# Second group's sigmoids as 1/(1+exp(-x)), with its first attention one to two beats later and the exponential's table loaded ahead

## The chip, the core and the metric

The kernel runs on one core of a Trainium2 chip. The metric is the device time of one execution in microseconds. Five engines work side by side, each through its own instruction list in order, and meet at semaphores: TensorE (PE, its weight loads PEld), VectorE (DVE), ScalarE (ACT), GpSimd (POOL) and SyncE (SP, DMA issues).

## What is computed

One pre-norm decoder layer over x of 32 batches x 128 tokens x 128 features, with a context of 32 x 128 x 96:

```python
x = x + attn(layernorm(x))            # linear attention, 16 heads
x = x + xattn(layernorm(x), ctx)      # softmax cross attention, 16 heads of 64
x = x + ffn(layernorm(x))             # shared SwiGLU + top-1 of 8 experts
# attn:
h = x @ Wh + bh;  v = x @ Wv + bv
q = sigmoid(x @ Wq + bq);  k = sigmoid(x @ Wk + bk)
kv = einsum('bndh,bnmh->bdmh', k, v)
num = einsum('bndh,bdmh->bnmh', q, kv)
den = einsum('bndh,bdh->bnh', q, k.sum(tokens))
out = relu((layernorm(num / den) * ln_w + ln_b) * (h + beta) @ Wo + bo)
```

## The kernel before

The 32 batches are eight **groups** of four. The first attention ("s1") is done for a whole group at once, in named steps; the cross attention is done batch by batch. The program's time is a list of **beats** (n, b), n from -7 to 31 and b from 0 to 3. In the four beats of n, batch n's probabilities are turned (the transposes, L1386) and batch n+1's scores and exponentials are made. Every engine's list is written out by the same loop over (n, b); what it issues in a beat, and in which order, is fixed there.

In a beat TensorE issues: the turn of a quarter of batch n's probabilities (`turn_probs`), products for v, q and k of coming batches, at b = 0 the scores of batch n+1 and the product of batch n-1's probabilities with V, at b = 2 the output product of batch n-1, and last the s1 steps of the beat. VectorE issues: the reciprocals of the softmax sums, the emptying of v and of half of the q and k banks, the row maxima (`row_max`, L860), and last its s1 steps. ScalarE issues the emptying of turned probabilities (L1117), four exponentials with sums for each quarter (`exp_chunk`, L1111), the other half of q and k, and last its s1 steps. GpSimd normalises probabilities (`norm_probs`, L599) and does s1's rsqrt by power, the normalisations, and the "gate terms".

The s1 steps of a group g run, in order of need: stats of x; rstd of x; normalise x; turn x; copy x^T and x^T low (a number is held as a high and a low part for the products); project first pair and second pair (h, k and v of two batches each into `hkv`); project q; sigmoids (ScalarE, on the k part of `hkv`, L1082, and from the bank of q into `qsT`, L1086); k^T v; mask; q k^T v; attention (VectorE: a reciprocal of the denominators L743, two products L745, and the statistics); rstd of attention; gating, first half (L756) and second half (L763); turn gated; copy gated^T; output; x1 (L775, L778 and statistics); rstd of x1; normalise x1; turn x1; x1^T high (ScalarE, L1092) and x1^T low (VectorE, L794). The last two feed the q products of the next pair of batches of the cross attention: for group 1 those of batches 4 and 5, first at beat (2, 0).

Tables `PE_S1`, `ACT_S1`, `DVE_S1` and `POOL_S1` give each step a place relative to the group's start; the dictionary `MOVED` overrides it. Group 0 runs before the cross attention starts. Group 1's s1 lies where the cross attention begins, at beats (-2, 3) to (1, 2). Groups 2 to 7 have theirs inside the steady cross attention.

Matmul results go to eight PSUM banks: four for the scores, four in a ring (`Ring`) that everything else takes in program order. A result can start only when the tenant four places before has been emptied, by VectorE or ScalarE.

`sigmoid` and `exp` are in different activation tables, so that ScalarE's list has an ACT_TABLE_LOAD at each change. `sh_gu_hi` (ScalarE, L1150) and `sh_gu_lo` (VectorE, L1011) are the parts of the feed-forward weights, first used at beat (6, 0). `stay_awake` (L1451) issues matmuls with no use for their result in the stretches before the cross attention.

Of the kernel before, what the change touches and what calls it, by code (L numbers as in the profile page):

```python
# [10 lines left out]
ALU = mybir.AluOpType  # L11
ACT = mybir.ActivationFunctionType
AX = mybir.AxisListType

P = 128


class Ring:
# [17 lines left out]
    def made(self, name):  # L36
        return self.ready, self.index[name] + 1
# [18 lines left out]
def decoder_layer(nc, x, ctx_in, Wh, bh, Wq, bq, Wk, bk, Wv, bv, beta, ln_w, ln_b, Wo, bo,  # L56
# [30 lines left out]
    with ctx:  # L87
        def sb(name, shape, dt=F32):
            return ctx.enter_context(nc.sbuf_tensor(name, shape, dt))

        def sem(name):
            return ctx.enter_context(nc.semaphore(name))
# [9 lines left out]
        wkvh_lo = sb("wkvh_lo", [P, 3 * D], F32R)  # L102
        wo = sb("wo", [P, D])
        bq_col = sb("bq_col", [P, 1])
        b_hkv = sb("b_hkv", [P, 3 * D])
        beta_bc = sb("beta_bc", [P, D])
        lnw_bc = sb("lnw_bc", [P, D])
# [153 lines left out]
        centred = [sem("x_centred"), sem("x1_centred")]  # L261
        normed = [sem("x_normalised"), sem("attention_gated"), sem("x1_normalised")]
        k_sig = sem("k_sigmoid")
        hi_in = [sem("ctxT_high_part"), sem("x1T_high_part")]
        gate_in = sem("gate_terms")
        x1_in = sem("x1_ready")
# [74 lines left out]
                 (0, "turn context"): (-6, 2), (0, "context high"): (-6, 2), (0, "context low"): (-6, 2),  # L341
                 (0, "residual"): (-3, 0),
                 (1, "stats of x"): None, (1, "rstd of x"): (-4, 2), (1, "normalise x"): (-4, 3),
                 (1, "turn x"): (-2, 3), (1, "copy x^T"): (-2, 3), (1, "x^T low"): (-2, 3),
                 (1, "project first pair"): (-1, 0), (1, "first pair"): (-1, 0),
                 (1, "project second pair"): (-1, 1), (1, "second pair"): (-1, 1)})

        def steps_at(table_, starts, n, b):

            return [(g, step) for g, a in enumerate(starts) for (slot, beat), step in table_.items()  # L350
                    if MOVED.get((g, step), (a + slot, int(beat))) == (n, b)]
# [326 lines left out]
        def _(dve):  # L678
# [28 lines left out]
            def s1(g, step):  # L707
# [15 lines left out]
                if step in ("first pair", "second pair"):  # L723
                    for u in ((1, 2) if step == "first pair" else (3, 4)):
                        ps = made(r1, (g, u))
                        if u == 1 and g > 0:

                            dve.wait_ge(gate_in, g)
                        nc.vector.tensor_tensor(hkv[:, u - 1, 0:3 * D], ps[:, 0:3 * D], b_hkv[:], ALU.add)\
                            .then_inc(r1.emptied["s1_dve"], 1)  # L730
                if step == "mask":
                    for u in (6, 7):
                        ps = made(r1, (g, u))
                        for j in range(2):
                            last = nc.vector.tensor_tensor(kvm[:, 2 * (u - 6) + j, :],
                                                           ps[:, j * KVW:(j + 1) * KVW], head_mask[:], ALU.mult)
                        last.then_inc(r1.emptied["s1_dve"], 1)
# [236 lines left out]
            for n in range(FIRST, B):  # L974
                for b in range(NC):
# [28 lines left out]
                    if (n, b) == (FIRST + 2, 2):  # L1004
# [1 line left out]
                        nc.vector.scalar_tensor_tensor(out=xwq_lo[:], in0=rawq, scalar=DH ** -0.5,  # L1006
                                                       in1=xwq_hi[:].bitcast(F32), op0=ALU.mult,
                                                       op1=ALU.subtract).then_inc(w_lo, 1)
                    if (n, b) == (-1, 3):
                        dve.wait_ge(wm_hi, 1)  # L1010
                        nc.vector.tensor_tensor(sh_gu_lo[:], rawgu, sh_gu_hi[:].bitcast(F32), ALU.subtract)\  # L1011
                            .then_inc(wm_lo, 1)
                    if (n, b) == (FIRST + 2, 2):
                        dve.wait_ge(w_hi, 3)
                        nc.vector.tensor_tensor(xwv_lo[:], rawv, xwv_hi[:].bitcast(F32), ALU.subtract)\
                            .then_inc(w_lo, 1)
                    for g, step in steps_at(DVE_S1, S1_AT, n, b):
                        if g == 0 and step == "first pair":
                            dve.wait_ge(consts, CONSTS_BIAS)
                        if g == 0 and step == "mask":  # L1020
                            dve.wait_ge(consts, CONSTS_S1)
                        s1(g, step)
# [48 lines left out]
        def _(act):  # L1071
            def made(ring, name):
                act.wait_ge(*ring.made(name))
                return ring.bank(name)

            def s1(g, step):
                if step == "copy x^T":
                    nc.scalar.copy(xnT_hi[:], made(r1, (g, 0))[:]).then_inc(xT_hi, 1)
                if step == "sigmoids":

                    act.wait_ge(*r1.freed((g, 4)))
                    nc.scalar.activation(hkv[:, :, D:2 * D], hkv[:, :, D:2 * D], ACT.Sigmoid).then_inc(k_sig, 1)  # L1082
                    ps = made(r1, (g, 5))
                    if g == 0:
                        act.wait_ge(bq_in, 16)
                    nc.scalar.activation(qsT[:], ps[:], ACT.Sigmoid, bias=bq_col[:]).then_inc(r1.emptied["s1_act"], 1)  # L1086
                if step == "copy gated^T":
                    nc.scalar.copy(gT[:], made(r1, (g, 10))[:]).then_inc(r1.emptied["s1_act"], 1)
                if step == "context high":
                    nc.scalar.copy(ctxT_hi[:, g % 2], made(r1, (g, 13))[0:DE, :]).then_inc(hi_in[0], 1)  # L1090
                if step == "x1^T high":
                    nc.scalar.copy(xn2T_hi[:, g % 2], made(r1, (g, 12))[:]).then_inc(hi_in[1], 1)  # L1092

            def ffn(g, step):
                ring = ffn_ring(g)
# [49 lines left out]
            nc.scalar.copy(wq_hi[:], rawq1).then_inc(w1_hi, 1)  # L1145
            for n in range(FIRST, B):
                for b in range(NC):
                    if (n, b) == (-1, 2):
                        act.wait_ge(wm_in, 16 * 4)
                        nc.scalar.copy(sh_gu_hi[:], rawgu).then_inc(wm_hi, 1)  # L1150
                    if live(n):
# [77 lines left out]
        def _(pe):  # L1229
# [28 lines left out]
            def s1(g, step):  # L1258
# [17 lines left out]
                if step == "project q":  # L1276
                    product3(claim(r1, (g, 5))[:], wq_hi[:], wq_lo[:], xnT_hi[:], xnT_lo[:]).then_inc(r1.ready, 1)
                if step == "k^T v":
                    pe.wait_ge(k_sig, g + 1)
                    for u in (6, 7):  # L1280
                        ps = claim(r1, (g, u))
                        for j in range(2):
                            b = 2 * (u - 6) + j
                            last = pe.matmul(ps[:, j * KVW:(j + 1) * KVW], hkv[:, b, D:2 * D], hkv[:, b, 2 * D:],
                                             start=True, stop=True)
                        last.then_inc(r1.ready, 1)
                if step == "q k^T v":

                    pe.wait_ge(*r1.freed((g, 5)))
                    for u in (8, 9):  # L1290
                        ps = claim(r1, (g, u))
                        pe.wait_ge(*r1.freed((g, u - 2)))
                        for j in range(2):
                            b = 2 * (u - 8) + j
                            last = pe.matmul(ps[:, j * KVW:(j + 1) * KVW], qsT[:, b * S:(b + 1) * S], kvm[:, b, :],
                                             start=True, stop=True)
                        last.then_inc(r1.ready, 1)
# [280 lines left out]
```

## Time and profile before

| | |
|---|---|
| median of 3 runs | 607.21 us (606.89 to 608.82) |
| the profiled execution's own time | 606.39 us |
| its span in the trace | 604.7 us |
| PE busy | 576.7 us (95%), 5479 matmuls |
| PEld busy | 528.7 us (87%) |
| DVE busy | 432.2 us (71%), 1210 instructions |
| ACT busy | 432.0 us (71%), 1514 instructions |
| POOL busy | 311.9 us (52%) |
| chain that ended last, by engine | PE 66%, ACT 16%, DVE 10% |
| ACT_TABLE_LOAD | L1111 x8 and L1082 x7 and L1142 x1, mean 1283 ns |

The busy shares are means over the whole span; matmuls overlap, and their ends are modelled. Start times are microseconds from the span's start. Where an engine runs back to back, the step from one start to the next is a little shorter than the busy length of an instruction. A row "x4" stands for four instructions in a row, with the time from the first start to the last end. The profiled execution is 1.7 us longer than its span.

### The profile page before, as it was taken

The page shows a single profiled execution, that of the slowest core. Times are in us where ns is not written, and L with a number is a line of the kernel's source. Part 1 is how long each engine was busy: PE and PEld are TensorE (multiplying, and loading weights), DVE is VectorE, ACT ScalarE, POOL GpSimd, SP SyncE. Part 2 cuts the span into 40 slices and gives each one's busy share as a digit, 9 for nine tenths or more (in the row PEclk, how much of TensorE's full clock was granted, in tenths as well). Part 3 has the DMA queues.
Part 4 walks back from the last instruction along what each step waited for, and adds up shares of the span by engine and source line. Part 5 has one row for each costly group of instructions (what it writes and reads, how often), then busy time and mean ns, then how long its engine had stood idle before and what let it go on. Part 6 is the DMA issues. An engine that isn't in the chain of part 4 may idle for free.

```text
span 604.7 us, 15181 instructions
## 1 busy us (share of the span) xinstructions
PE 576.7 (95%) x5479; PEld 528.7 (87%) x5479; DVE 432.2 (71%) x1210; ACT 432.0 (71%) x1514; POOL 311.9 (52%) x332
## 2 busy tenths in 40 slices
PE   8978999999999999999999999999999999899993
PEld 8867998988999899989998889989998988788993
DVE  4869666877685858776876787767856558589773
ACT  2668778786877777677867687768777876665881
POOL 3545553365336643675347525655464326445774
PEclk9999999999999999999999999999999999999997
DMA  6530000100010000010000000000220201242530
GB/s 158 141 65 14 18 3 1 31 2 2 1 33 17 21 2 14 19 38 1 14 20 27 11 5 11 19 19 3 89 70 20 66 8 36 82 129 76 150 103 19
DMA packets 24955, 23.52 MB, mean 39 GB/s; under 512 B 7007, under 2 KB 22497, under 8 KB 24880
## 3 DMA queue, kind: packets, MB, share of 16 engines
q1 hardware_dynamic: 21520, 15.96, 10.2%
q0 software_dynamic: 2784, 6.32, 3.0%
q8 instruction: 45, 0.74, 0.5%
q10 hardware_dynamic: 576, 0.26, 0.2%
q14 instruction: 30, 0.25, 0.1%
HBM read 15.03 MB, written 7.95 MB: 38 GB/s over the span
## 4 chain that ended last, share of the span: by engine, by line
PE 66%; ACT 16%; DVE 10%; issue 2%; POOL 2%; DMA 2%; SPq 1%; POOLq 0%; DVEq 0%; ACTq 0%
PE bank L1408 8%; PE bank L1376 8%; PE bank L1397 8%; PE bank L1386 7%; PE bank L1237 7%; ACT prob L1111 7%; PE bank L1239 6%; PE bank L1238 6%; PE bank L1522 4%; PE bank L1539 2%; PE bank L1255 2%; PE bank L1357 2%; ACT probT L1117 2%; DMA prob<-in_L_xattn_Wk_dram 2%; PE bank L1243 1%
## 5 line engine op out<-in xcount | busy, mean ns | idle before, releaser
L1111 ACT ACTIVATE prob<-bank,mneg 128x128 f32<-128x128 f32 x512 | 183.4, 388 | 63.3 <-DVE mneg L860 63.1
L599 POOL TENSOR_TENSOR prob<-prob,rden 128x512 f32<-128x512 f32 x128 | 131.1, 1045 | 104.2 <-DVE rden L867 104.0
L1111 ACT ACTIVATION_READ_ACCUMULATOR prob<-bank,mneg 128x1 f32 x512 | 115.8, 226 | 0.0
L1117 ACT COPY probT<-bank 128x512 f32<-128x512 f32 x128 | 77.9, 609 | 19.3 <-PE bank L1386 18.7
L860 DVE TENSOR_REDUCE mneg<-bank 128x4 f32<-128x512 f32 x128 | 83.1, 670 | 2.5 <-PE bank L1376 2.5
L1386 PE MATMUL bank<-ident,prob 128*128 128x128 f32 x512 | 78.6, 276 | 3.4 <-POOL prob L599 2.0
L538 POOL TENSOR_TENSOR rstd<-var_eps,neg_half 128x4 f32<-128x4 f32 x24 | 24.7, 1030 | 97.5 <-DVE var_eps L694 97.5
L1386 PEld LDWEIGHTS bank<-ident,prob 128*128 128x128 f32 x512 | 59.6, 142 | 10.5 <-ACT probT L1117 3.1
L1376 PE MATMUL bank<-kT,qT 64*128 64x128 f32 x1024 | 66.2, 279 | 0.4 <-ACT prob L1111 0.4
L1376 PEld LDWEIGHTS bank<-kT,qT 64*128 64x128 f32 x1024 | 59.8, 188 | 6.3 <-issue 2.5
L1408 PE MATMUL bank<-xwo,oT 128*128 128x128 f32 x512 | 63.7, 277 | 0.5 <-ACT oT L1121 0.5
L877 DVE COPY V<-bank 128x512 f32<-128x512 f32 x62 | 42.8, 690 | 29.6 <-PE bank L1239 28.4
L1397 PE MATMUL bank<-probT,V 128*64 128x128 f32 x1024 | 63.0, 276 | 0.0
L1408 PEld LDWEIGHTS bank<-xwo,oT 128*128 128x128 f32 x512 | 59.8, 192 | 2.9 <-ACT qT L1131 1.2
L1397 PEld LDWEIGHTS bank<-probT,V 128*64 128x64 f32 x1024 | 55.2, 137 | 4.0 <-issue 0.3
L1522 PE MATMUL bank<-oT,qT 128*128 128x128 f32 x312 | 41.1, 275 | 0.0
L1522 PEld LDWEIGHTS bank<-oT,qT 128*128 128x128 f32 x312 | 38.0, 192 | 0.2
L591 POOL DMA_INDIRECT routed<-record,row_i x32 | 32.7, 1022 | 7.9 <-issue 4.8
L1121 ACT COPY oT<-bank 128x512 f32<-128x512 f32 x64 | 35.6, 601 | 1.2 <-PE bank L1397 0.3
L1237 PE MATMUL bank<-xwv_hi,ctxT_hi 96*128 96x512 f32 x64 | 30.7, 480 | 1.4 <-ACT oT L1121 1.3
L1131 ACT COPY qT<-bank 128x512 f32<-128x512 f32 x32 | 19.7, 616 | 16.5 <-PE bank L1239 16.5
L1237 PE MATMUL bank<-xn2T_hi,xwq_hi 128*128 128x256 f32 x96 | 28.9, 301 | 0.9 <-DVE V L877 0.6
(224 smaller groups left out, 1389.7 us busy)
## 6 DMA issues: line engine op xcount, KB each, us to landing
prob<-routed SPq DMA_DIRECT2D x39, 128.5 KB, 2.2
s_work<-in_x_dram SPq DMA_DIRECT2D x8, 256.0 KB, 2.9
ctx_nat<-in_ctx_dram SPq DMA_DIRECT2D x8, 192.0 KB, 2.7
routed<-blank SPq DMA_DIRECT2D x9, 128.5 KB, 4.1
s_work<-in_L_ffn_rt_gate_dram SPq DMA_DIRECT2D x1, 1024.0 KB, 5.5
s_work<-in_L_ffn_rt_up_dram SPq DMA_DIRECT2D x1, 1024.0 KB, 9.5
prob<-in_L_xattn_Wq_dram SPq DMA_DIRECT2D x1, 512.0 KB, 6.9
xwo<-in_L_xattn_Wo_dram SPq DMA_DIRECT2D x1, 512.0 KB, 9.2
```

Source lines behind the costliest of these rows:

```text
L599: nc.gpsimd.tensor_tensor(view, view, spread(rden[:, m % 2, c * NC:(c + 1) * NC], 2, S), ALU.mult)\
L860: nc.vector.tensor_reduce(mneg[:, m % 2, c * NC:(c + 1) * NC], score_bank[c][:].rearrange("p (h k) -> p h k", k=S), AX.X, ALU.max, negate= ...
L877: nc.vector.tensor_copy(V[:, m % 2, half * 512:(half + 1) * 512], ps[:])\
L1111: last = nc.scalar.activation(prob[:, m % 2, p * S:(p + 1) * S], score_bank[c][:, i * S:(i + 1) * S], ACT.Exp, bias=mneg[:, m % 2, p:p + 1 ...
L1117: nc.scalar.copy(probT[:, m % 2, c * 512:(c + 1) * 512], made(r1, ("T", m, c))[:])\
L1237: pe.matmul(ps, w_hi_, t_hi, start=True, stop=False)
L1238: pe.matmul(ps, w_hi_, t_lo, start=False, stop=False)
L1376: last = pe.matmul(score_bank[2 * j + half][:, i * S:(i + 1) * S], qT[rows, pair % 2, 4 * j + i, cols], kT[rows, pair % 2, 4 * j + i, cols ...
L1386: last = pe.transpose(ps[:, i * S:(i + 1) * S], prob[:, m % 2, p * S:(p + 1) * S], ident[:])
L1397: last = pe.matmul(ps[DH * half:DH * half + DH, i * S:(i + 1) * S], V[:, m % 2, h * DH:(h + 1) * DH], probT[:, m % 2, p * S:(p + 1) * S], ...
L1408: last = pe.matmul(ps[:, 0:D], oT[:, m % 2, k * S:(k + 1) * S], xwo[:, k, :], start=(k == 0), stop=(k == NK - 1))
L1522: last = pe.matmul(gu_bank[(j - 1) % 3][:, c * P:(c + 1) * P], w4[(j - 1) % 3][:, c * P:(c + 1) * P], recT[:, (j - 1) % 2], start=True, st ...
```

## The change

For group 1 alone the sigmoids become exponentials on ScalarE (of -x, the q bias negated in advance into `bq_neg`), and VectorE adds 1 and takes the reciprocal: two passes over 128x512 for k, two for q, in a step of its own, "second sigmoids", at beat (-1, 3). TensorE's k^T v and q k^T v of group 1 wait for the semaphore of that step. An exponential of 128x4 with no use for its result stands behind group 0's "x1^T high". Steps of group 1 are moved later (before, where they had no entry of their own, the tables gave the places in the second column):

| step of group 1 | before | after |
|---|---|---|
| x^T low | (-2, 3) | (-1, 0), behind two row maxima |
| sigmoids (ACT) | (-1, 1) | (-1, 2) |
| second sigmoids (DVE) | none | (-1, 3) |
| k^T v; mask | (-1, 2) | (0, 0) |
| gate terms (POOL) | (-1, 1) | (0, 0) |
| q k^T v; attention; rstd of attention | (-1, 3) | (0, 1) |
| gating, first and second half | (0, 0), (0, 1) | (0, 2) |
| turn gated; copy gated^T | (0, 2) | (0, 3) |
| output; x1; rstd of x1 | (0, 3) | (1, 0) |
| normalise x1 | (1, 0) | (1, 1) |
| turn x1; x1^T high; x1^T low | (1, 2) | (1, 3) |

`sh_gu_hi` goes from beat (-1, 2) to (-2, 2), `sh_gu_lo` from (-1, 3) to (1, 2). Groups 0 and 2 to 7 keep the sigmoid.

```diff
@@ MOVED
-                 (1, "turn x"): (-2, 3), (1, "copy x^T"): (-2, 3), (1, "x^T low"): (-2, 3),
+                 (1, "turn x"): (-2, 3), (1, "copy x^T"): (-2, 3), (1, "x^T low"): (-1, 0),
...
+                 (1, "sigmoids"): (-1, 2), (1, "k^T v"): (0, 0), (1, "mask"): (0, 0), (1, "q k^T v"): (0, 1),
+                 (1, "attention"): (0, 1), (1, "gate terms"): (0, 0), (1, "rstd of attention"): (0, 1),
+                 (1, "gating, first half"): (0, 2), (1, "gating, second half"): (0, 2),
+                 (1, "turn gated"): (0, 3), (1, "copy gated^T"): (0, 3), (1, "output"): (1, 0), (1, "x1"): (1, 0),
+                 (1, "rstd of x1"): (1, 0), (1, "normalise x1"): (1, 1), (1, "turn x1"): (1, 3),
+                 (1, "x1^T high"): (1, 3), (1, "x1^T low"): (1, 3)})
@@ VectorE
+                if step == "second sigmoids":
+                    dve.wait_ge(exp_1, 1)
+                    v = hkv[:, :, D:2 * D]
+                    link(nc.vector.tensor_scalar(v, v, 1.0, None, ALU.add))
+                    nc.vector.reciprocal(v, v).then_inc(sig_1, 1)
+                    dve.wait_ge(*r1.freed((g, 5)))
+                    link(nc.vector.tensor_scalar(qsT[:], qsT[:], 1.0, None, ALU.add))
+                    nc.vector.reciprocal(qsT[:], qsT[:]).then_inc(sig_1, 1)
...
-                    if (n, b) == (-1, 3):
+                    if (n, b) == (1, 2):
                         dve.wait_ge(wm_hi, 1)
...
+                    if (n, b) == (-1, 3):
+                        s1(1, "second sigmoids")
@@ ScalarE
+                if step == "sigmoids" and g == 1:
+                    act.wait_ge(*r1.freed((g, 4)))
+                    nc.scalar.activation(hkv[:, :, D:2 * D], hkv[:, :, D:2 * D], ACT.Exp, scale=-1.0).then_inc(exp_1, 1)
+                    ps = made(r1, (g, 5))
+                    act.wait_ge(bq_turned, 1)
+                    nc.scalar.activation(qsT[:], ps[:], ACT.Exp, scale=-1.0, bias=bq_neg[:])\
+                        .then_inc(r1.emptied["s1_act"], 1)
...
+                    if g == 0:
+                        nc.scalar.mul(bq_neg[:], bq_col[:], -1.0).then_inc(bq_turned, 1)
...
                     nc.scalar.copy(xn2T_hi[:, g % 2], made(r1, (g, 12))[:]).then_inc(hi_in[1], 1)
+                    if g == 0:
+
+                        nc.scalar.activation(table_first[:], neg_half[:], ACT.Exp)
...
-                    if (n, b) == (-1, 2):
+                    if (n, b) == (-2, 2):
                         act.wait_ge(wm_in, 16 * 4)
@@ TensorE
-                    pe.wait_ge(k_sig, g + 1)
+                    if g == 1:
+                        pe.wait_ge(sig_1, 1)
+                    else:
+                        pe.wait_ge(k_sig, max(g, 1))
...
-                    pe.wait_ge(*r1.freed((g, 5)))
+                    pe.wait_ge(*((sig_1, 2) if g == 1 else r1.freed((g, 5))))
```

## Rows read from the trace of the kernel before

**Rows 1.** Busy time by engine from 57.3 us to the last matmul. Columns: start and end, length, engines, TensorE clock
```profile
57.30:595.00 537.70, 527.53 (x5110) 484.22 (x5110) 390.94 (x1084) 398.46 (x1425) 281.72 (x280) 1.00 0.11 33
```

**Rows 2.** Chain that ended last, 38 to 46 us. Columns: start, length (us), engine, output, line
```profile
38.91 0.69 DVE mneg L860
...
39.62 2.90 ACT prob L1111 x16
...
42.53 1.28 ACT L1082
...
43.83 0.64 ACT s_work L1082
```

**Rows 3.** ScalarE in order of time, 35 to 46 us. Start, length, instruction, idle before
```profile
35.68 0.59 ACT L1131 COPY qT<-bank 128x512 f32<-128x512 f32 x1 [2.10 <-PE bank L1239]
37.12 0.58 ACT L1131 COPY qT<-bank 128x512 f32<-128x512 f32 x1 [0.85 <-PE bank L1239]
...
44.94 0.61 ACT L1150 CAST sh_gu_hi<-x 128x512 fp32r<-128x512 f32 x1
```

**Rows 4.** TensorE in order of time, 44 to 66 us
```profile
44.51 1.25 PE L1284 MATMUL bank<-s_work 128*128 128x144 f32 x8 [2.03 <-ACT s_work L1082]
...
47.03 0.60 PE L1386 MATMUL bank<-ident,prob 128*128 128x128 f32 x4
...
56.64 0.66 PE L1255 MATMUL bank<-ident,s_work 128*128 128x128 f32 x4 [0.67 <-DVE s_work L763]
57.24 0.66 PE L1386 MATMUL bank<-ident,prob 128*128 128x128 f32 x4
...
59.31 1.06 PE L1307 MATMUL bank<-wo,qsT 128*128 128x128 f32 x8
...
65.33 0.66 PE L1386 MATMUL bank<-ident,prob 128*128 128x128 f32 x4
```

**Rows 5.** VectorE in order of time, 45 to 57 us
```profile
45.31 1.01 DVE L735 TENSOR_TENSOR kvm<-bank,head_mask 128x144 f32<-128x144 f32 x4 [1.48 <-PE bank L1284]
46.24 1.05 DVE L1011 TENSOR_TENSOR sh_gu_lo<-x,sh_gu_hi 128x512 fp32r<-128x512 f32 x1
47.21 0.34 DVE L743 RECIPROCAL rden<-bank 128x32 f32<-128x32 f32 x1
...
50.29 0.20 DVE L867 RECIPROCAL rden<-den 128x8 f32<-128x8 f32 x1
50.41 0.64 DVE L872 COPY qT<-bank 128x512 f32<-128x512 f32 x1
50.96 1.28 DVE L860 TENSOR_REDUCE mneg<-bank 128x4 f32<-128x512 f32 x2
52.16 2.06 DVE L756 SCALAR_TENSOR_TENSOR s_work<-s_work,mv 128x128 f32<-128x128 f32 x4
...
55.45 1.13 DVE L763 SCALAR_TENSOR_TENSOR s_work<-s_work,rstd 128x128 f32<-128x128 f32 x4
56.50 0.68 DVE L789 TENSOR_TENSOR ctxT_lo<-bank,ctxT_hi 96x512 fp32r<-96x512 f32 x1
```

**Rows 6.** VectorE groups by line and shape. Columns: operation, count, busy us, mean ns, idle
```profile
L867 DVE RECIPROCAL rden<-den 128x8 f32<-128x8 f32 x64 | 12.5, 196 | 7.0 <-ACT prob L1111 6.4
...
L743 DVE RECIPROCAL rden<-bank 128x32 f32<-128x32 f32 x16 | 5.7, 354 | 3.0 <-PE bank L1295 3.0
...
L839 DVE TENSOR_TENSOR rank<-bank,next_row 128x32 f32<-128x32 f32 x8 | 1.5, 183 | 0.0
```

**Rows 7.** TensorE in order of time, 70 to 71.3 us
```profile
70.42 0.60 PE L1255 MATMUL bank<-ident,xn 128*128 128x128 f32 x4
```

**Rows 8.** ScalarE in order of time, 72.5 to 73.3 us
```profile
72.90 0.58 ACT L1131 COPY kT<-bank 128x512 f32<-128x512 f32 x1 [0.57 <-PE bank L1239]
```

**Rows 9.** TensorE in order of time, 590 to 605 us: its last matmuls
```profile
595.14 0.71 PE L1539 MATMUL bank<-kT,V 128*128 x4 [0.64 <-DVE V L1039]
```

**Rows 10.** Granted clock after the last matmul of the program
```profile
597.00:598.00 1.00, 0.00 (x0) 0.00 (x0) 0.00 (x0) 0.00 (x0) 0.69 (x2) 0.59 0.02 0
```

More of the change, by code:

```diff
@@ L104, in decoder_layer @@
         bq_col = sb("bq_col", [P, 1])
+        bq_neg = sb("bq_neg", [P, 1])
         b_hkv = sb("b_hkv", [P, 3 * D])
@@ L263, in decoder_layer @@
         k_sig = sem("k_sigmoid")
+        bq_turned = sem("q_bias_negated")
+        exp_1 = sem("second_group_exponentials")
+        sig_1 = sem("second_group_sigmoids")
         hi_in = [sem("ctxT_high_part"), sem("x1T_high_part")]
@@ L343, in decoder_layer @@
                  (1, "stats of x"): None, (1, "rstd of x"): (-4, 2), (1, "normalise x"): (-4, 3),
-                 (1, "turn x"): (-2, 3), (1, "copy x^T"): (-2, 3), (1, "x^T low"): (-2, 3),
+                 (1, "turn x"): (-2, 3), (1, "copy x^T"): (-2, 3), (1, "x^T low"): (-1, 0),
                  (1, "project first pair"): (-1, 0), (1, "first pair"): (-1, 0),
-                 (1, "project second pair"): (-1, 1), (1, "second pair"): (-1, 1)})
+                 (1, "project second pair"): (-1, 1), (1, "second pair"): (-1, 1),
+                 (1, "sigmoids"): (-1, 2), (1, "k^T v"): (0, 0), (1, "mask"): (0, 0), (1, "q k^T v"): (0, 1),
[4 more added lines that the diff above has]
+                 (1, "x1^T high"): (1, 3), (1, "x1^T low"): (1, 3)})
         def steps_at(table_, starts, n, b):
@@ L1078, in s1 @@
                     nc.scalar.copy(xnT_hi[:], made(r1, (g, 0))[:]).then_inc(xT_hi, 1)
-                if step == "sigmoids":
+                if step == "sigmoids" and g == 1:
[5 more added lines that the diff above has]
+                        .then_inc(r1.emptied["s1_act"], 1)
+                if step == "sigmoids" and g != 1:
                     act.wait_ge(*r1.freed((g, 4)))
```

## The prediction

> **What bounds the kernel now.** I read the busy time by stretch first. From 57.3 us to the last matmul TensorE is busy 527.5 of 537.7 us at full clock [rows 1]: what delays its list there by a microsecond delays the end by one, for nothing idle follows that could take it up. So the change is worth what it does to TensorE's position by the time the steady stretch starts. Ahead of that the bound changes. In the chain, ScalarE's first eight exponentials are followed by a table load, then by k's sigmoid, which TensorE's k^T v awaits [rows 2]; TensorE's own list shows the 2.03 us pause ahead of k^T v [rows 4]. VectorE's list from 45.3 us on is then without a gap, and TensorE waits for it again, 0.67 us, at turn gated [rows 4, 5]. VectorE is thus the next to be late, and the change gives it more work there.
>
> My marker is the start of the turn of batch 1's second quarter, at 65.33 us before [rows 4]. The same work must be done ahead of it in both kernels.
>
> **ScalarE's edits.** The exponential's early load (1.28 us) falls into an idle time of 2.10 us, `sh_gu_hi` at its new place (0.61 us) into one of 0.85 us [rows 3]; both are hidden, and without that cover would hold back the q copies behind them by their length. The negated bias is one tiny copy in group 0's idle start: nothing. x^T low goes behind two row maxima: the maxima come some 0.3 us earlier, the first pair 0.3 us later. The third exponential chunk waits for its row maximum, which is behind the first pair, until about 42.5; so the earlier start is not kept. Two of the chunks took 2.90 us [rows 2]. k's exponential is behind the third chunk: 42.5 + 1.45 + 0.65 = **44.6 us**, and it is only the input of the new VectorE step. k's sigmoid was done at 44.47 before [rows 2], so the removed load (1.28) has been spent on the chunk put ahead.
>
> Here row and page differ. The row has the load at 42.53 and the sigmoid at 43.83, so a switch costs 1.28 us and nothing after it [rows 2]. The Trainium skill, "ScalarE: Activation LUTs", What ACT_TABLE_LOAD costs, adds a drain of about 1.38 us to each; with it the two removed switches would free ScalarE for 5.3 instead of 2.6 us. The trace speaks against it, and ScalarE isn't the bound in what follows.
>
> **The new VectorE step.** Two additions and two reciprocals over 128x512. An addition is like any pass of that size, 0.65 (0.6 to the 1.05 of `sh_gu_lo`, both operands of which are in SBUF) [rows 5]. No reciprocal of that size is in the trace. It has one of 8 elements at 196 ns and one of 32 at 354 ns, while a product of 32 elements takes 183 ns [rows 6]. So the reciprocal costs by the element: (354 - 196)/24 = 6.6 ns, 196 + 504 x 6.6 = 3.5 us; or the excess over the product, 171/32 = 5.3 ns, x 512 + 0.65 = 3.4 us. The lower bound is a plain pass, 0.65; the upper takes the whole of the longer row as cost by the element, 354/32 = 11 ns, which gives 5.7 us. I take **3.4 us**, since both rows point there. The step is 2 x (0.65 + 3.4) = 8.1 us, and ends at 44.6 + 8.1 = **52.7 us**.
>
> The rule on this is in the Trainium skill, "VectorE: DVE Perf Modes", the 8-slice pipeline: reciprocal iterates with a repeat count of 8. Eight times the 1.05 ns an element of a plain pass would be 4.3 us, and the sum 1.8 us longer.
>
> **What is queued behind it.** In VectorE's order, with the start-to-start steps of [rows 5]: reciprocal of the sums 0.1, q copy 0.55, two row maxima 1.2, mask 0.95, V copy 0.6, row maximum 0.6, attention with its statistics 3.1 (47.21 to 50.29), context low 0.6, reciprocal, row maximum and q copy 1.3, gating 2.1 and 1.1. Together 12.2 us; gated values at **64.9 us**. TensorE keeps ahead of each: it waits for the q copy at 53.4 before the v product (the copy frees a bank), for the mask and the ring at q k^T v, for context low at the next v product. ScalarE's exponentials of batch 1 begin at 54, after the maximum.
>
> Turn gated was at 56.64, and from there TensorE ran back to back to the marker, 8.7 us. The turn, v and q products of beat (0, 3) (57.24 to 59.31, 2.1 us) are now ahead of turn gated, the output behind the scores and the product with V. What remains is 6.6 us [rows 4]: marker at 64.9 + 6.6 = 71.5, which is **6.2 us late**. That `sh_gu_lo` and the mask leave their old place is in this walk and counts no second time.
>
> **Behind the marker.** (a) x1 (two passes of 0.7 and statistics like those of attention, some 2.85 us) now begins at 71.5 and the V copy is behind it, so the output product of batch 0 waits for its bank: 71.5 + 2.85 + 0.6 = 74.95, while TensorE arrives at 74.4: 0.5 us. (b) Turn x1 was at 70.42, more than two microseconds before the k copy of 72.90 [rows 7, 8]. Now it is behind that k product, and x1^T high is on ScalarE behind k copy and an exponential chunk: 0.5 + 1.4 + 0.5 = 2.4 us, beside TensorE's two turns of 0.85. With x1^T low (0.7, against the 0.5 of products that need only the high part) the q product of beat (2, 0) waits **1.9 us**. This does not depend on the reciprocals.
>
> Moved otherwise: GpSimd's gate terms leave the way of the first normalisation, so the first turn comes before its 47.03 [rows 4]; that is lost again at the q copy's bank. SyncE's load of the third group's x waits for x1_in, so is issued some 11 us later, for use much further on: nothing.
>
> **Sum:** 6.2 + 0.5 + 1.9 = 8.6 us. 606.39 + 8.6 = 615.0; the median of the runs shown is 0.8 above the profiled execution, so **615.8 us**.
>
> **Rivals.** (1) Reciprocals are plain passes. Step 2.6 us, end at 47.3; VectorE's 12.2 then has some 0.6 of waits for TensorE: gated at 60.0, marker 66.6, 1.3 late, with (a) and (b) 3.7: 610.9. For it: nothing but the missing row; against it the 354 to 183 ns. Chance 0.10.
>
> (2) TensorE's clock falls. After k^T v (to 49.9) and one turn it idles from 50.3 to 53.4. After the last matmul of the program, which ended at 595.85, the granted clock was at full until the second from 597.0 to 598.0, whose mean is 0.59, between 2.4 and 1.2 GHz [rows 9, 10]: a pause of some 2 us was enough there. The v, q and q k^T v products that VectorE awaits (2.1 us) would take twice as long: 617.9 at most. Against: VectorE is behind on its own work, so much of that is hidden. Chance 0.13.
>
> (3) It is faster: the pause of 2.03 us goes, and nothing takes its place: 604.4, with the 0.8 605.2. Place: the marker, which must come before 65.3. It decides at turn gated, which must be ready by 65.3 - 6.6 = 58.7, so that VectorE's step ends by 46.5: 1.9 us for four passes. Even then (b) costs 1.9. It needs passes at under 0.5 us and the k copy, exponentials and x1^T high hidden. Chance 0.04.
>
> (4) The exponential's table stays loaded where it was, as the early activation doesn't bring it ahead. The load was hidden behind the row maximum (ready at 39.60, exponential at 39.62) [rows 2], so this changes nothing: 615.8, in the forecast's chance.
>
> **The numbers.** Forecast 0.70, 613 to 618 by itself (reciprocals at 2.9 to 4.3 us give -1.0 to +1.8). Passes partly hidden so that the time stays within 0.3% (1.8 us, about what a measurement of this kernel can tell from no change) 0.03. Range: down to rival 1 less a little, up to rival 2 with the longer reciprocals: 609.8 to 619.0. Slower takes forecast, rivals 1 and 2: 0.93.
>
> **What would show it.** Two reciprocals of 128x512 near 3.4 us on VectorE, ending near 52.7; TensorE's k^T v at about 48.8 and then pauses; turn gated at 64.9; marker at 71.5; a wait of almost 2 us for x1^T high near 80; then the old list 8 to 9 us late to the end, with TensorE's sum of work unchanged. Wrong would be: reciprocals under 1 us, a marker before 66, or no wait for x1^T high.

## The result and the profile after

The changed kernel takes 617.16 us (median of 4 executions, 616.99 to 619.04), the kernel before 607.47 in the same runs. The ratio is 1.0167, 95% interval [1.0143, 1.0190]: slower by 9.7 us. The forecast was 615.8, the range 609.8 to 619.0. The spans of the two profiled executions are 615.3 and 604.7 us, 10.6 us apart.

VectorE in order of time, changed kernel. Columns: start, busy length, engine, line, operation, idle before:

```profile
45.04 0.43 DVE L746 TENSOR_SCALAR s_work<-s_work 128x512 f32<-128x512 f32 x1 [0.50 <-ACT s_work L1103]
45.50 3.35 DVE L747 RECIPROCAL s_work<-s_work 128x512 f32<-128x512 f32 x1
48.77 0.36 DVE L749 TENSOR_SCALAR qsT<-qsT 128x512 f32<-128x512 f32 x1
49.17 3.35 DVE L750 RECIPROCAL qsT<-qsT 128x512 f32<-128x512 f32 x1
52.44 0.14 DVE L887 RECIPROCAL rden<-den 128x8 f32<-128x8 f32 x1
52.50 0.63 DVE L892 COPY qT<-bank 128x512 f32<-128x512 f32 x1
...
61.30 2.04 DVE L776 SCALAR_TENSOR_TENSOR s_work<-s_work,mv 128x128 f32<-128x128 f32 x4
63.38 1.14 DVE L783 SCALAR_TENSOR_TENSOR s_work<-s_work,rstd 128x128 f32<-128x128 f32 x4
```

The new step takes 7.5 us, from 45.0 to 52.5. Its first row waits 0.50 us for ScalarE's exponential; behind it no row in the list down to the gated values at 64.5 has any idle time ahead of it. The gating passes that answer to [rows 5] were at 52.16 and 55.45.

TensorE, who waited for whom, 40 to 90 us of the changed kernel. Columns: waiting instruction, releaser, us in total, times, longest:

```profile
PE bank L1289 <- DVE s_work L783: 2.7, 1, 2.7
PE bank L1423 <- POOL prob L611: 2.0, 1, 2.0
PE bank L1277 <- ACT xn2T_hi L1123: 1.8, 1, 1.8
PE bank L1271 <- DVE qT L892: 1.4, 1, 1.4
...
PE bank L1445 <- DVE V L897: 0.6, 1, 0.6
```

TensorE in order of time, changed kernel:

```profile
64.57 1.12 PE L1289 MATMUL bank<-ident,s_work 128*128 128x128 f32 x4 [2.72 <-DVE s_work L783]
...
73.66 0.60 PE L1423 MATMUL bank<-ident,prob 128*128 128x128 f32 x4
...
77.44 2.05 PE L1445 MATMUL bank<-xwo,oT 128*128 128x128 f32 x16 [0.63 <-DVE V L897]
...
83.99 0.36 PE L1277 MATMUL bank<-xn2T_hi,xwq_hi 128*128 128x256 f32 x1 [1.77 <-ACT xn2T_hi L1123]
```

The marker of the prediction, the turn of batch 1's second quarter, is at 73.66, against 65.33 in [rows 4]: 8.33 us late. Behind it stand the two new waits, 0.63 us for the output product's bank and 1.77 us for x1^T high. 8.33 + 0.63 + 1.77 = 10.7 us, which is the difference of the spans (10.6) but for 0.1.

The profiled executions don't all reach this part of the program at the same time. The first q copy on ScalarE, which no edit delays, starts at 35.68 us in the kernel before [rows 3] and at 35.95 in the changed kernel, so 0.27 of the 8.33 us are a later start. In other runs it starts up to 1.5 us later; where it bears on a comparison below, it is given.

TensorE needs 9.1 us from turn gated to the marker, where the same instructions took 6.6 before (65.33 - 56.64, less the 2.07 us of products that now stand ahead of turn gated [rows 4]). The changed kernel's busy time by stretch says why (columns as in [rows 1]; the third from the end is the granted clock):

```profile
46.00:48.00 2.00, 2.00 (x15) 1.78 (x16) 2.00 (x1) 1.45 (x7) 0.37 (x1) 0.51 0.00 0
...
62.00:64.00 2.00, 0.00 (x0) 0.00 (x0) 1.96 (x6) 1.88 (x9) 0.67 (x1) 0.78 0.00 0
64.00:66.00 2.00, 1.43 (x7) 1.43 (x8) 1.23 (x4) 0.27 (x1) 0.69 (x1) 0.50 0.00 0
66.00:68.00 2.00, 2.00 (x11) 1.78 (x11) 0.14 (x1) 0.90 (x2) 1.34 (x2) 0.50 0.00 0
68.00:70.00 2.00, 2.00 (x20) 2.00 (x22) 0.69 (x2) 0.00 (x0) 0.00 (x0) 0.52 0.00 0
```

TensorE is idle from 61.9 to 64.6, its clock falls to 1.2 GHz in that pause, and it runs at half until about 70: 2.5 us of the lateness. It is at half from 46 to 49.5 us too, behind the 2.0 us pause of the first turn; there TensorE waits for VectorE afterwards in any case, 1.4 us for the q copy.

So the loss of the profiled execution is the start's 0.3 us and four terms of the change: turn gated 5.6 us late by VectorE's list, 2.5 us half clock, 0.6 us a bank, 1.8 us x1^T high.

### The profile page after: what moved, and what is told of

Read it like the earlier page. It is cut to its first block, busy times and chain, and to the rows that moved or that the text cites. A ratio compares the mean times of both kernels' runs of the same rounds, so it can differ in the third digit from the quotient of the medians.

```text
span 615.3 us, 15187 instructions
## 1 busy us (share of the span) xinstructions
PE 580.3 (94%) x5479; PEld 532.0 (86%) x5479; DVE 439.5 (71%) x1214; ACT 430.5 (70%) x1514; POOL 312.4 (51%) x332
## 4 chain that ended last, share of the span: by engine, by line
PE 66%; ACT 15%; DVE 12%; issue 2%; DMA 2%; POOL 2%; SPq 1%; POOLq 0%; DVEq 0%; ACTq 0%
PE bank L1413 8%; PE bank L1445 8%; PE bank L1434 7%; PE bank L1423 7%; ACT prob L1145 7%; PE bank L1271 7%; PE bank L1273 6%; PE bank L1272 5%; PE bank L1559 4%; PE bank L1289 2%; PE bank L1576 2%; PE bank L1394 2%; DMA prob<-in_L_xattn_Wk_dram 2%; ACT probT L1151 2%; PE bank L1277 2%
## 5 line engine op out<-in xcount | busy, mean ns | idle before, releaser
L1413 PE MATMUL bank<-kT,qT 64*128 64x128 f32 x1024 | 68.1, 285 | 0.0
L1413 PEld LDWEIGHTS bank<-kT,qT 64*128 64x128 f32 x1024 | 62.0, 194 | 6.0 <-issue 3.0
```

The costliest lines, as they stand in the source:

```text
L1413: last = pe.matmul(score_bank[2 * j + half][:, i * S:(i + 1) * S], qT[rows, pair % 2, 4 * j + i, cols], kT[rows, pair % 2, 4 * j + i, cols ...
```

## The experiments

Times of the first four stand against 607.33 us of the kernel before, of the next four against 607.30, of the last four against 607.09.

### Eighteen wake matmuls in the pause ahead of turn gated

```diff
+                    if (n, b) == (0, 3):
+                        pe.wait_ge(exp_done, NC + 1)
+                        stay_awake(18)
```

> The changed kernel with 18 matmuls of no use (120 ns each, 2.2 us) in TensorE's pause of 2.7 us ahead of turn gated. Theory (the half clock from 64 to 69.5 us is a cost of its own): the clock stays at 2.4 GHz, the marker (turn of batch 1's second quarter, 73.66) comes near 71.4, the time is about 2.3 us under the changed kernel's 617.2, at 614.9. Rival (VectorE and the chain of waits set the pace there, the half clock is covered): within 0.3 us of 617.2.

619.28 us, 1.0186 [1.0165, 1.0207]. A miss. The 18 matmuls show as 36 instructions in the trace:

```profile
63.74 4.18 PE L1488 MATMUL bank<-ident 128*128 128x128 f32 x36
67.76 0.60 PE L1289 MATMUL bank<-ident,s_work 128*128 128x128 f32 x4
```

The clock stays full there, and turn gated to marker takes 74.32 - 67.76 = 6.6 us. But turn gated is 3.2 us later than in the changed kernel. 0.8 us of it is a later start. 1.2 us is the wake matmuls, which end after the gated values are ready (66.6). The remaining 1.2 us has a cause ahead of the edit, where the instructions are those of the changed kernel: here the clock stays full at the first turn and falls at the next pause.

```profile
53.98 0.50 PE L1271 MATMUL bank<-xwv_hi,ctxT_hi 96*128 96x512 f32 x1 [2.60 <-DVE qT L892]
...
57.05 2.09 PE L1332 MATMUL bank<-kvm,qsT 128*128 128x144 f32 x8
```

```profile
56.00:58.00 2.00, 2.00 (x11) 2.00 (x10) 1.17 (x2) 2.00 (x11) 1.97 (x2) 0.50 0.04 8
```

Q k^T v takes 2.09 us instead of 1.15, and VectorE's attention (58.24) waits 1.07 us for it. This is what rival 2 of the prediction described. At the marker these two terms of 1.2 us use up the 2.5 us that the full clock gives. The clock falls once more from 86.25 to 89.75 us, behind the wait for x1^T high; the start and this fall are the 2.3 us by which this span exceeds the changed kernel's. The run says nothing on the net worth; it was repeated with ten, below.

### Without q's reciprocal

```diff
-                    link(nc.vector.tensor_scalar(qsT[:], qsT[:], 1.0, None, ALU.add))
-                    nc.vector.reciprocal(qsT[:], qsT[:]).then_inc(sig_1, 1)
+                    nc.vector.tensor_scalar(qsT[:], qsT[:], 1.0, None, ALU.add).then_inc(sig_1, 1)
```

> The changed kernel without q's reciprocal (q is left as 1+exp(-x), so this part of the computation is changed). Theory (VectorE's list is in series from the new step to turn gated): the step ends 3.35 us earlier, near 49.2, turn gated near 61.2, the time 3.3 us under 617.2, at 613.9 with the clock still falling in the pause, near 611.7 if the pause ahead of turn gated gets short enough. Rival (ScalarE's exponentials or the PSUM ring hold TensorE, and VectorE is late beside them): under 1 us gained, over 616.2.

613.68 us, 1.0104 [1.0089, 1.0118]: 3.5 us under the changed kernel, for a reciprocal of 3.35 us. The profiled execution is the slowest of the four (616.07; the others 613.30 to 614.00). TensorE in it:

```profile
61.25 1.11 PE L1288 MATMUL bank<-ident,s_work 128*128 128x128 f32 x4 [2.73 <-DVE s_work L782]
...
70.78 0.60 PE L1422 MATMUL bank<-ident,prob 128*128 128x128 f32 x4
```

Turn gated moves from 64.57 to 61.25, by 3.32 us, and the pause ahead of it stays 2.7 us, so the half clock comes again (9.5 us to the marker). Up to turn gated the series on VectorE holds one for one. At the end only 1.0 us of it is left in this execution, as the clock falls again at the wait for x1^T high and is at half until 84.75:

```profile
82.00:84.00 2.00, 2.00 (x16) 1.78 (x16) 0.69 (x1) 0.00 (x0) 1.99 (x2) 0.50 0.02 4
```

The mean granted clock of the other three is 0.989 to 0.992, of this one 0.986; they spent less time at half, and no trace shows where. That the medians differ by the length of the reciprocal is thus partly luck.

### Turn x1 back by one beat

```diff
-                 (1, "rstd of x1"): (1, 0), (1, "normalise x1"): (1, 1), (1, "turn x1"): (1, 3),
-                 (1, "x1^T high"): (1, 3), (1, "x1^T low"): (1, 3)})
+                 (1, "rstd of x1"): (1, 0), (1, "normalise x1"): (1, 1), (1, "turn x1"): (1, 2),
+                 (1, "x1^T high"): (1, 2), (1, "x1^T low"): (1, 2)})
```

> The changed kernel with turn x1, x1^T high and x1^T low of group 1 back at beat (1, 2). Theory (the 1.77 us wait for x1^T high comes from its place behind the exponentials): that wait goes, but turn x1 now waits for GpSimd's normalisation, which ended at 80.1 where TensorE arrives near 79.3: net 0.8 to 1.2 us under 617.2, at 616.2. Rival (the x1 chain is late as such, and the wait only changes its name): within 0.3 us of 617.2.

615.89 us, 1.0142 [1.0123, 1.0161]: 1.3 us under the changed kernel. TensorE's waits in this run have no x1^T high, and instead:

```profile
PE bank L1289 <- POOL xn L557: 0.7, 1, 0.7
```

1.77 - 0.68 = 1.1 us, as expected: most of that wait came from the place of the step and not from a late x1.

### All moves, with ScalarE's sigmoid

```diff
-                    nc.scalar.activation(hkv[:, :, D:2 * D], hkv[:, :, D:2 * D], ACT.Exp, scale=-1.0).then_inc(exp_1, 1)
+                    nc.scalar.activation(hkv[:, :, D:2 * D], hkv[:, :, D:2 * D], ACT.Sigmoid).then_inc(sig_1, 1)
...
-                    nc.scalar.activation(qsT[:], ps[:], ACT.Exp, scale=-1.0, bias=bq_neg[:])\
+                    nc.scalar.activation(qsT[:], ps[:], ACT.Sigmoid, bias=bq_col[:])\
...
-                    if (n, b) == (-1, 3):
-                        s1(1, "second sigmoids")
```

> All of the moves kept, but group 1's sigmoids done by ScalarE as before, so no additions and reciprocals on VectorE and two table loads back. Theory (the moved places cost by themselves, the reciprocals come on top): ScalarE's last chunk of batch 0 ends near 49.5 instead of 46.5, VectorE goes on from there instead of 52.4, everything some 3 us earlier; with the clock not falling late 5 us: 612 to 614.3, still clearly over the kernel before at 607.4. Rival (the reciprocals are the whole loss): within 1 us of 607.4.

617.65 us, 1.0161 [1.0145, 1.0178] (one execution of the six took 1972 us and is left out of the ratio; without it the median is 617.51). Both the theory's 612 to 614.3 and the rival's 607.4 are missed: without any reciprocal it is as slow as the changed kernel. ScalarE and TensorE of this run, in order of time, and the stretch between them:

```profile
44.65 1.28 ACT L1101 ACT_TABLE_LOAD   x1
...
47.17 1.28 ACT L1143 ACT_TABLE_LOAD   x1
```

```profile
50.02 2.08 PE L1411 MATMUL bank<-kT,qT 64*128 64x128 f32 x16 [1.17 <-ACT prob L1143]
52.03 1.85 PE L1319 MATMUL bank<-s_work 128*128 128x144 f32 x8
```

```profile
48.00:50.00 2.00, 0.85 (x8) 0.56 (x6) 0.00 (x0) 1.99 (x10) 0.00 (x0) 0.50 0.00 0
50.00:52.00 2.00, 1.98 (x16) 1.79 (x16) 1.95 (x4) 1.05 (x4) 1.71 (x2) 0.50 0.00 0
```

The loads hold the last exponentials of batch 0 back to 49.9, the second half of batch 1's scores waits for them, and all of it runs at half clock, so that k^T v is at 52.03 (50.06 in the changed kernel) and gating ends at 64.5 again. VectorE idles 5.3 us here instead of doing reciprocals. What had been left out of the expectation is the half clock and the scores' wait for the last exponentials. The half clock holds from 46.25 to 53.5 us, longer than in the changed kernel. In these places the table loads and the half clock together thus cost as much as the reciprocals; how it divides between the two was not separated. What the moves cost without either is shown further down.

### Ten wake matmuls

```diff
-                        stay_awake(18)
+                        stay_awake(10)
```

> The changed kernel with 10 wake matmuls ahead of turn gated. In the first try 18 of them showed as 36 instructions and took 4.2 us, longer than the pause; 10 take 2.3 us of the 2.7. Theory (the half clock after the pause costs by itself): the clock stays full from 62 us on, turn gated to the marker takes 6.6 us instead of 9.1, the time is 2 to 2.5 us under 617.2. Rival (the lost half clock is paid elsewhere, as the clock falls at another pause): within 1 us of 617.2.

615.79 us, 1.0136 [1.0119, 1.0152]: 1.4 us under the changed kernel, between theory and rival. TensorE of this run:

```profile
61.03 2.39 PE L1488 MATMUL bank<-ident 128*128 128x128 f32 x20
63.92 0.66 PE L1289 MATMUL bank<-ident,s_work 128*128 128x128 f32 x4 [0.49 <-DVE s_work L783]
...
70.53 0.60 PE L1423 MATMUL bank<-ident,prob 128*128 128x128 f32 x4
```

Turn gated to marker takes 6.6 us. The marker is 3.1 us earlier than in the changed kernel, 0.7 us of it by an earlier start and 2.5 us by the clock. But now the clock falls behind the wait for x1^T high:

```profile
82.00:84.00 2.00, 2.00 (x25) 1.98 (x26) 1.25 (x2) 0.00 (x0) 1.76 (x2) 0.70 0.01 4
84.00:86.00 2.00, 2.00 (x22) 1.78 (x20) 1.93 (x11) 1.51 (x8) 0.00 (x0) 0.50 0.03 8
```

In the changed kernel's own trace the same wait of 1.77 us brought no fall. So both hold: the half clock at turn gated is a cost of its own, 2.5 us at the marker, and in this execution a part of it is paid at another pause, as the rival said.

### Tanh in the moved places

`v` and `qsT` become tanh(x/2) + 1, twice the sigmoid; the factor cancels between numerator and denominator. `bq_neg` holds half the bias.

```diff
-                    nc.scalar.activation(hkv[:, :, D:2 * D], hkv[:, :, D:2 * D], ACT.Exp, scale=-1.0).then_inc(exp_1, 1)
+                    nc.scalar.activation(hkv[:, :, D:2 * D], hkv[:, :, D:2 * D], ACT.Tanh, scale=0.5).then_inc(exp_1, 1)
...
-                    link(nc.vector.tensor_scalar(v, v, 1.0, None, ALU.add))
-                    nc.vector.reciprocal(v, v).then_inc(sig_1, 1)
+                    nc.vector.tensor_scalar(v, v, 1.0, None, ALU.add).then_inc(sig_1, 1)
```

(q alike.)

> All of the moves kept; group 1's sigmoids as tanh(x/2) + 1, twice the sigmoid: the factor is in numerator and denominator alike and cancels. Tanh needs no table switch here, VectorE has two additions (0.85 us) and no reciprocal. Theory (reciprocals 6.7 us of VectorE's series; without them and without table loads TensorE's order takes over): turn gated near 60, marker near 66.3, then the waits of 0.6 and 1.8 us: 609.5 to 611. Rival (the moves cost the same whatever stands for the sigmoid, as the run with ScalarE's sigmoid in the moved places could be read): 616 to 618.

614.27 us, 1.0117 [1.0101, 1.0133]: a miss, between theory and rival. The profiled execution, 612.25, is the fastest of the four. In it:

```profile
60.11 1.12 PE L1287 MATMUL bank<-ident,s_work 128*128 128x128 f32 x4 [2.74 <-DVE s_work L781]
...
68.65 0.60 PE L1421 MATMUL bank<-ident,prob 128*128 128x128 f32 x4
```

```profile
60.00:62.00 2.00, 1.89 (x9) 1.90 (x10) 0.77 (x3) 0.58 (x1) 1.16 (x2) 0.50 0.00 0
```

Turn gated is at 60.1 as expected, then the half clock puts the marker at 68.65 instead of 66.3. That is 2 us of the miss; the other executions of this kernel are 2 us longer still, and no trace shows where.

### Reciprocals at the places of before

```diff
-                 (1, "sigmoids"): (-1, 2), (1, "k^T v"): (0, 0), (1, "mask"): (0, 0), (1, "q k^T v"): (0, 1),
...
-                    if (n, b) == (-1, 3):
-                        s1(1, "second sigmoids")
...
                         s1(g, step)
+                        if g == 1 and step == "second pair":
+                            s1(1, "second sigmoids")
```

(All entries of group 1 that the change added or altered in `MOVED` are undone; `sh_gu_hi` and `sh_gu_lo` keep their new places.)

> Exponentials and reciprocals for group 1, but every step of group 1 at its place of before, and the new VectorE step directly behind second pair. Theory (VectorE's series is what counts, wherever it stands): the step ends near 50.6, the reciprocal of the softmax sums and GpSimd's first normalisation wait for it, TensorE's first turn is at 52 to 53 instead of 47.0: 5 to 8 us over the kernel before, 612.5 to 615.5. It is under the changed kernel's 617.2 since the 2.4 us of waits behind the marker are absent. Rival (the moves hide the reciprocals and without them it is much worse): over 617.2.

615.4 us, 1.0132 [1.0116, 1.0148]: inside the expected range. TensorE of this run:

```profile
48.73 2.29 PE L1314 MATMUL bank<-s_work 128*128 128x144 f32 x8 [5.75 <-DVE s_work L740]
53.53 2.26 PE L1325 MATMUL bank<-kvm,qsT 128*128 128x144 f32 x8 [2.51 <-DVE kvm L748]
55.58 1.01 PE L1416 MATMUL bank<-ident,prob 128*128 128x128 f32 x4
...
73.18 0.66 PE L1416 MATMUL bank<-ident,prob 128*128 128x128 f32 x4
```

TensorE waits 5.75 us for k's reciprocal and 2.5 us for the mask, at half clock from 46 to 56.5; its first turn is at 55.58, later than the 52 to 53 expected, and the marker (73.18) about where the changed kernel has it. Behind the marker the 2.4 us of waits are gone, and one of 0.95 us for x1^T low is new, which the new place of `sh_gu_lo` makes. The places that the change gives the steps therefore gain nothing even for the reciprocals; they cost 1.8 us more.

### Tanh at the places of before

The edit of "tanh in the moved places", made in the kernel before: additions ahead of the mask at beat (-1, 2), exponential's table loaded early.

```diff
+                        if step == "mask" and g == 1:
+                            s1(g, "plus one")
```

> The kernel before with group 1's sigmoids as tanh(x/2) + 1 (the factor of 2 cancels) at the places of before, and the table loaded early: both table loads of the stretch gone, 0.85 us more on VectorE. Theory (VectorE's gapless list sets turn gated, ScalarE's loads matter only until k^T v): k^T v 0.2 us earlier, then VectorE as late as before: 0.5 us gained to 0.7 lost, 606.8 to 608. Rival (the loads in the chain are worth their length): 604.8.

607.49 us over 12 executions, 1.0005 [0.9996, 1.0013]: no difference, as the theory had it. Two table loads of 1.28 us leave ScalarE, two additions of 2.4 us together come to VectorE, and the exchange is worth nothing; k^T v now waits for the addition and starts at 44.65 (44.51 before [rows 4]). What the loads alone are worth isn't shown. VectorE's row of q's addition and the stretch behind it:

```profile
44.52 1.49 DVE L740 TENSOR_SCALAR qsT<-qsT 128x512 f32<-128x512 f32 x1
```

```profile
48.00:50.00 2.00, 2.00 (x11) 1.99 (x11) 1.85 (x8) 0.59 (x1) 0.37 (x1) 0.50 0.00 0
```

The addition takes 1.49 us here and 0.36 in the changed kernel, and the clock is at half from 47 to 50.5. Mask and turn gated are at 45.93 and 57.24, later than the 45.31 and 56.64 of [rows 4, 5].

### The moves alone, with the clock kept up

The kernel of "tanh in the moved places", with the ten wake matmuls and turn x1 back at beat (1, 2).

> tanh_moved with 10 wake matmuls ahead of turn gated and turn x1 with both parts back at beat (1, 2): the moves alone, without reciprocals, and with the clock and the x1^T high wait taken out. Theory (tanh_moved's 614.3 was the moves plus a half clock at one or two pauses): turn gated to marker 6.6 us, marker near 66.5, waits of 0.6 and 0.7 behind it: 609 to 610.5. Rival (the clock is not what brought tanh_moved from the expected 610 to 614): over 612.

610.29 us, 1.0051 [1.0036, 1.0066], inside the range. The granted clock is 1.00 in every stretch from 40 to 88 us. TensorE:

```profile
61.12 0.66 PE L1287 MATMUL bank<-ident,s_work 128*128 128x128 f32 x4 [0.49 <-DVE s_work L781]
...
67.73 0.60 PE L1421 MATMUL bank<-ident,prob 128*128 128x128 f32 x4
```

It is 4.0 us under "tanh in the moved places"; the rows show 3.0 of it, 1.9 by the clock ahead of the marker and 1.1 by the wait for x1^T high. And it is 3.2 us over the kernel before, with no reciprocal, no table load, no half clock and no wait for x1^T high. The trace has the marker 2.4 us late, 1.0 of it by a later start of this execution, and behind it the waits of 0.6 for the output product's bank and 0.7 for turn x1. The wake matmuls hold nothing back: TensorE still waits 0.49 us for VectorE behind them. So some 3 us are what the later places cost by themselves, with turn x1 in its beat of before. Which of the moves costs how much was not separated.

### Lighter lists, with the sigmoid kept

```diff
-                 (1, "project second pair"): (-1, 1), (1, "second pair"): (-1, 1)})
+                 (1, "project second pair"): (-1, 1), (1, "second pair"): (-1, 1),
+                 (1, "gate terms"): (-1, 2)})
...
-                    if (n, b) == (-1, 3):
+                    if (n, b) == (1, 2):
                         dve.wait_ge(wm_hi, 1)
...
-                    if (n, b) == (-1, 2):
+                    if (n, b) == (-2, 2):
                         act.wait_ge(wm_in, 16 * 4)
```

> The kernel before with only VectorE's and GpSimd's lists made lighter there: the parts of the shared gate and up weights at the changed kernel's places, gate terms one beat later at (-1, 2) behind the normalisation; sigmoids by ScalarE as before. Theory (VectorE is the next to be late in the kernel before): sh_gu_lo's 0.97 us leave its list, attention some 0.5 us earlier, turn gated near 56.0: 0.4 to 1.0 us gained, 606.3 to 606.9. Rival (ScalarE's loads bound it): 607.3.

607.9 us over 11 executions, 1.0014 [1.0005, 1.0023]: a miss, a little slower. VectorE and TensorE in order of time:

```profile
70.98 1.65 DVE L1012 TENSOR_TENSOR sh_gu_lo<-x,sh_gu_hi 128x512 fp32r<-128x512 f32 x1
72.55 0.68 DVE L795 TENSOR_TENSOR xn2T_lo<-bank,xn2T_hi 128x512 fp32r<-128x512 f32 x1
```

```profile
56.10 0.66 PE L1256 MATMUL bank<-ident,s_work 128*128 128x128 f32 x4 [0.67 <-DVE s_work L764]
...
73.28 0.66 PE L1387 MATMUL bank<-ident,prob 128*128 128x128 f32 x4 [0.93 <-DVE xn2T_lo L795]
```

Turn gated is at 56.10, 0.54 us earlier, as expected (0.1 of it by the start). But `sh_gu_lo`, at its new place 1.65 us long, now stands ahead of x1^T low in the same beat, and TensorE waits 0.93 us. In the changed kernel x1^T low is a beat later, and no wait for it is in its trace.

### Tanh with lighter lists, and the same with wake matmuls

The edits of "tanh at the places of before" and of the lighter lists together; then the same with `stay_awake(6)` ahead of k^T v.

> tanh_1 (tanh(x/2) + 1 for group 1, no table switches) with the lighter lists. In tanh_1 the two additions took 0.94 and 1.49 us beside GpSimd's gate terms, against 0.43 and 0.36 with GpSimd idle, and sh_gu_lo stood behind them. Theory: additions near 0.45 each, attention near 46.3, turn gated near 55.5, the clock perhaps half from 46 to 50: 605 to 606.5, the first version under the kernel before. Rival (nothing there is worth time, as tanh_1 showed): 607.3.

607.96 us over 11 executions, 1.0017 [1.0008, 1.0026].

> tanh_light with 6 wake matmuls (12 instructions, 1.4 us) in TensorE's pause ahead of k^T v. Theory: the clock does not fall there in any execution, 0.3 to 1.2 us under tanh_light, 604.5 to 605.5. Rival (TensorE has slack there, the half clock is covered by VectorE): equal to tanh_light within 0.3 us.

607.73 us over 11 executions, 1.0009 [0.9997, 1.0020]. Both miss: neither is under the kernel before. The wait of 0.9 us for x1^T low is in both. The additions still took 0.81 and 1.26 us beside GpSimd's normalisation. Without the wake matmuls the clock is at half from 45 to 48.75 us, and VectorE waits 0.37 and 0.59 us for TensorE there; turn gated is at 57.37, not at the 55.5 expected. With them the clock is full throughout. That execution starts 1.46 us later, by which k^T v is at 46.17 instead of 44.71; less this, its turn gated (58.09) is 0.7 us earlier. The medians are 0.2 us apart, which is within the spread. No version beat the kernel before.

## Why the prediction was right, point by point

- **VectorE next to be late, and in series.** Right. The step was put at 44.6 to 52.7 and is at 45.0 to 52.5; the 12.2 us behind it were 12.1; turn gated was put at 64.9 and is at 64.57. The run without q's reciprocal shows the series one for one up to turn gated.
- **The reciprocal by the element.** 3.4 us forecast, 3.35 measured, 6.5 ns an element, from two rows of 8 and 32 elements. The prediction's estimate from the repeat count of 8 in the Trainium skill ("VectorE: DVE Perf Modes", the 8-slice pipeline) was 4.3; the trace doesn't bear it out. The additions were over-sized: 0.43 and 0.36 us against 0.65 each. This and the start of the step, 0.4 us later than forecast (0.27 of it the later start of the execution), about cancel.
- **The two waits behind the marker.** 0.5 and 1.9 forecast, 0.63 and 1.77 measured. The run with turn x1 put back shows that most of the second is of the place.
- **Hidden edits.** Right: table load at 33.87 and `sh_gu_hi` at 36.43 lie in ScalarE's idle time. The load was brought ahead, so rival 4 didn't occur.
- **The clock.** This is the term that the forecast's sum lacks, and the marker (71.5 forecast, 73.66 measured) is late by it. Rival 2 had the mechanism, with 0.13, at the pause from 50.3 to 53.4 and with the reason against it that VectorE would cover it. The row that it rested on was read too long: the last matmul ends at 595.85, and a mean clock of 0.59 in the second from 597.0 [rows 10] puts the fall near 597.2, 1.3 us behind it and not 2. In the changed kernel's trace the falls came at two other pauses, the first turn's and turn gated's; in the run with 18 wake matmuls one came at rival 2's own pause, and VectorE covered all but 1.07 us. The first fall stretched the scores from 2.06 to 3.28 us, which is why k^T v is at 50.06 and not at the 48.8 forecast, at no cost to the marker. At the second TensorE is the one that everybody waits for, so nothing covers it: 2.5 us of its own list. The step that failed is that the pause ahead of turn gated, which the walk gives (idle from the last q product to 64.9), was not read as a pause for the clock. That the forecast of 615.8 lies within 1.4 us of 617.16, though it lacks 2.5 us, is in part luck. Turn gated came 0.3 us earlier than forecast. And the 0.8 us added for the distance of the median from the profiled execution was not there in the changed kernel, whose profiled execution took 617.10.
- **The moves as a loss in their own right.** The forecast had this only in its parts: the two waits behind the marker, of which it said that the second doesn't depend on the reciprocals, and the walk of rival 1, 3.7 us in all with cheap passes. The run with the moves alone, turn x1 put back, puts them at 3.2 us. The forecast didn't ask what the reciprocals cost without the moves: with every step at its old place the kernel is 1.8 us faster than the changed one.

Open is why the clock falls at one pause of 1.8 to 2.0 us and not at another of the same length, or at the same pause in another execution (below), and the remaining 2 us between the profiled and the other executions of "tanh in the moved places".

## What to carry to other kernels

Before an activation is rebuilt on VectorE, price its reciprocal by the element (here 6.5 ns, so 6.7 us for the two, against the 2.6 us of two table loads) and look whether VectorE's list has a gap there at all; tanh(x/2) + 1 in a ratio does the same for two additions and the exponential's table, here without a loss at the old places, but without a gain either (607.49 against 607.30 us). A step that is moved later on all engines needs its consumers checked, as here x1^T high behind a chunk of exponentials just ahead of its product. And for a new wait of 2 us or more on TensorE the half clock of what it does next is a term to price, here 1.9 to 2.9 us between turn gated and the marker behind pauses of 2.7 us.

## What was not expected of the hardware

- The clock at pauses of TensorE: after 2.03 us of idle ahead of k^T v it stayed full in the trace before. Around the pause of 2.04 us ahead of the first turn it fell in the changed kernel and stayed full in the run with 18 wake matmuls, though the two have the same instructions up to there. Around the wait of 1.77 us for x1^T high it fell in three traces (18 and ten wake matmuls, and without q's reciprocal) and stayed full in three (the changed kernel, "tanh in the moved places", ScalarE's sigmoid). Around turn gated's pause of 2.7 us it fell in every trace that had this pause without wake matmuls: in the changed kernel 1.3 us into it, in "tanh in the moved places" at its very start, behind a shorter pause of 1.37 us. The falls in these traces last from 3.5 to 10.5 us.
- An addition of 128x512 in SBUF took 0.36 us with GpSimd idle, and up to 1.49 us in stretches where GpSimd was at work; yet one of 0.43 us lay beside GpSimd's normalisation. `sh_gu_lo` took 0.68 us ("tanh at the places of before") and 1.05 us (before) beside that normalisation, and 1.65 us (lighter lists) beside GpSimd's addition for `x1b`. Which pairs of operations hold each other up was not separated.
- Of ScalarE's table load, the traces have 1.28 us and the next activation directly behind it, here too (44.65 and 45.95 in the run with all moves and ScalarE's sigmoid).
